# One quarter of a state-space product moved from VectorE to GpSimd, and the first expert tile fetched in the routing stage, in a fused Mamba, attention and mixture-of-experts kernel

## The chip, the cores and the metric

The kernel runs on one NeuronCore of a Trainium2 chip. The metric is the device time of one execution in microseconds (us); lower is better. In the text PE is TensorE, DVE is VectorE, ACT is ScalarE, POOL is GpSimd and SP is SyncE, which here only issues DMAs. SBUF is the on-chip memory of 128 partitions, PSUM the accumulators that TensorE writes.

## The reference

All arrays are float32. The input is x, 2 sequences of 2048 rows of 256. It is normalised, and the output is x plus the sum of two branches. Cut to what matters:

```python
# branch 1: state-space layer (512 inner channels, 16 states)
dA  = jnp.exp(jnp.einsum('bld,dn->bldn', dt, A))
dBx = jnp.einsum('bld,bln->bldn', dt, Bm) * xs[..., None]
h   = dA_t * h + dBx_t                      # a scan over the 2048 rows
y   = jnp.einsum('bdn,bn->bd', h, C_t)
out = ((y + xs * D) * jax.nn.silu(res)) @ W_out

# branch 2: attention (16 heads of 16), then one of 8 experts per row
x   = x + (o @ wo + bo)
hn2 = _layernorm(x, ln2_g, ln2_b)
idx = jnp.argmax(hn2 @ gate_w + gate_b, axis=-1)
y   = relu(hn2 @ w1[idx] + b1[idx]) @ w2[idx] + b2[idx]
return x + y
```

## The kernel before

The kernel is one program of five stages, one after the other, each a block with its own instruction stream for every engine: projections, the state-space layer, attention, routing, experts. Engines signal each other by semaphores. A stage ends when all engines have ended theirs. The order of the work on every engine is written out by hand.

**State-space stage (`phase_mamba`).** The 4096 rows are 8 chunks of 512. In a chunk there are 16 units k: unit k = (q, j) holds four states (group q of 4) of 128 channels (tile j of 4). All its tiles are 128 partitions (channels) by 4 x 512 (states by rows). One unit goes through the engines like this:
- POOL makes DB = B rows times U (dt times x), L1138, one unit or more ahead. Before that it makes the carry HS of the unit that DVE has finished (L1112), so it waits for DVE's product of unit k-2 (`hc_done`).
- ACT makes the decays exp(dt*A) for one state at a time into PSUM (L1243), two buffers deep.
- DVE runs four scans into H (L1521), then the product G = H * C rows over all four states (L1534), which signals `hc_done`. G, H and DB have two buffers each.
- PE adds the four states up in PSUM by four matmuls with the identity (L1387), which signals `y_done`.

In units 11 to 15 POOL also issues six DMAs that add into DT in memory (`add_steps`, L1124) and so form the next chunk's dt; some of them wait until an earlier one has landed. DVE makes U = dt * x for the next chunk in units 14 and 15 (L1480), and the gating product of one channel tile, read from PSUM, in units 13 to 15 and in unit 0 of the next chunk (L1488). PE runs the convolutions and projections of the next chunk in between. SP loads the rows of B and C, spread over all partitions (`load_b`, `load_c`).

**Routing stage (`phase_route`).** POOL first builds the identity and SEL, a 16 x 256 mask that spreads the softmax sums over the channels (L1663 to L1668). For each of 8 chunks PE projects, DVE normalises and picks the expert, and POOL scatters the rows' ids into the table ids_d, sorted by expert (L1688). Then DVE works out TE and TR, the expert and the first table row of each of 23 tiles (L1867 to L1884), and POOL waits until all scatters have landed.

**Expert stage (`phase_experts`).** For each tile of 256 rows SP loads ids, W1, B1, W2 and BB by the numbers in TE and TR (L1936 to L1955), POOL gathers the rows by the ids (L1981), PE transposes them (L2010) and multiplies by W1 (L2025) and W2 (L2038). Two buffers of weights, three of rows, four of ids. The stage begins with six memsets of the row buffers on DVE, for which the first gathers wait.

In the attention stage (`phase_attention`) POOL starts with memsets and six loads of weights, waits for them, and then has the first of 32 small casts (L756).

## Time and profile before

| | |
|---|---|
| median of 3 runs | 3058.38 us (3058.3 to 3058.73) |
| profiled execution | 3059.3 us, of which the span from the first to the last instruction is 3057.6 us |
| mean granted clock of PE | 0.959 of full speed |
| busy, share of the span | PE 93%, DVE 83%, ACT 57%, POOL 33% |
| state-space stage | about 190 to 1150 us |
| attention, routing, experts | from about 1163, 2582 and 2704 us |

The stages follow one another, so a change in one is worth what it does to that stage's own length. The profile gives every instruction with its start, its duration and, where its engine was idle before it, what ended the wait. A row that holds several instructions of one kind ends with their number.

### The profile page before, as it was taken

To read this page: it belongs to the slowest core of one execution; us is meant where nothing else is said; L and a number is where in the kernel's file an instruction comes from. 1 tells how busy PE (TensorE), PEld (TensorE's weight loads), DVE (VectorE), ACT (ScalarE), POOL (GpSimd) and SP (SyncE) were. 2 spreads that over 40 slices of the span, in tenths; PEclk is the share of its full clock that TensorE was granted. 3 is DMA by queue.
4 is the path that set the end of the run, shared out by engine and by line. 5 is a ranking of instruction groups with operands and counts; after the bars stand their busy time and mean duration, and the time that the engine had idled before them with its cause. 6 is when DMAs were issued, how large, how long until landed. Compare 5 with 4: busy or idle time off the path is not lost. (4 is left out here: it accounts for less than half of the span.)

```text
span 3057.6 us, 36491 instructions
## 1 busy us (share of the span) xinstructions
PE 2847.3 (93%) x13168; PEld 1457.7 (48%) x13168; DVE 2543.2 (83%) x4091; ACT 1757.2 (57%) x2146; POOL 1001.2 (33%) x652
## 2 busy tenths in 40 slices
PE   7988999989999668999999999999999998959998
PEld 4533434434434234444444444444444442758887
DVE  7569999999999997899999999999999993732222
ACT  4457567566676530677777777777777776111110
POOL 3337667666666753011010110101000000444443
PEclk9999999999999885899999999999999999779999
DMA  7624244343352526554465545655455501546663
GB/s 239 215 90 111 83 117 108 93 117 105 92 129 79 122 54 89 65 76 75 62 88 74 76 75 63 88 74 76 75 63 74 74 11 39 123 144 200 206 201 108
DMA packets 193968, 310.11 MB, mean 101 GB/s; under 512 B 97613, under 2 KB 133990, under 8 KB 179324
## 3 DMA queue, kind: packets, MB, share of 16 engines
q1 hardware_dynamic: 176380, 260.12, 39.9%
q0 software_dynamic: 17408, 47.66, 6.6%
q8 instruction: 104, 1.70, 0.2%
q14 instruction: 76, 0.62, 0.1%
HBM read 237.10 MB, written 53.52 MB: 95 GB/s over the span
## 5 line engine op out<-in xcount | busy, mean ns | idle before, releaser
L895 DVE TENSOR_REDUCE attn_mx<-attn_pX 128x1 f32<-128x512 f32 (+1 forms) x2560 | 1308.0, 576 | 52.7 <-PE attn_pX L798 14.7
L869 ACT ACTIVATE attn_pr<-attn_pS 128x1024 f32<-128x1024 f32 x1024 | 991.6, 1021 | 410.5 <-PE attn_pS L810 410.5
L798 PE MATMUL attn_pX<-attn_ks,attn_qs 48*128 48x512 f32 (+1 forms) x1920 | 660.9, 430 | 6.1 <-DVE attn_mx L895 5.1
L1521 DVE TENSOR_TENSOR_SCAN mamba_h<-mamba_pA,mamba_hs,mamba_db 128x512 f32<-128x512 f32 x512 | 616.8, 1264 | 13.0 <-ACT mamba_pA L1243 12.6
L1387 PE MATMUL mamba_pY<-mamba_g,mamba_ident 128*128 128x512 f32 x1024 | 498.0, 631 | 107.6 <-DVE mamba_g L1534 107.4
L1138 POOL TENSOR_TENSOR mamba_db<-mamba_bq,mamba_u 128x2048 f32<-128x2048 f32 x128 | 580.6, 4537 | 11.6 <-DVE mamba_u L1480 11.6
L798 PEld LDWEIGHTS attn_pX<-attn_ks,attn_qs 48*128 48x128 f32 x1920 | 327.9, 186 | 466.9 <-DVE attn_mx L895 412.4
L1243 ACT ACTIVATE mamba_pA<-mamba_dt,held_an 128x512 f32<-128x512 f32 x512 | 352.1, 690 | 295.2 <-DVE mamba_h L1521 292.5
L810 PE MATMUL attn_pS<-attn_qs,attn_ks 50*128 50x512 f32 x1536 | 466.0, 434 | 2.8 <-ACT attn_pr L869 2.8
L820 PE MATMUL attn_pO<-attn_pr,attn_vs 128*17 128x512 f32 x3072 | 404.2, 598 | 0.8 <-ACT attn_pr L869 0.7
L1387 PEld LDWEIGHTS mamba_pY<-mamba_g,mamba_ident 128*128 128x128 f32 x1024 | 194.0, 199 | 403.2 <-issue 203.7
L756 POOL CAST attn_ms<-attn_mn 128x16 fp32r<-128x16 f32 x32 | 6.3, 198 | 1146.9 <-DVE attn_mn L903 996.1
L1534 DVE TENSOR_TENSOR mamba_g<-mamba_h,mamba_bq 128x2048 f32<-128x2048 f32 x128 | 297.6, 2325 | 11.8
L798 PE MATMUL attn_pX<-item_ks,item_qs 48*128 48x512 f32 (+1 forms) x640 | 231.6, 460 | 11.4 <-DVE attn_mx L895 5.1
L810 PEld LDWEIGHTS attn_pS<-attn_qs,attn_ks 50*128 50x128 f32 x1536 | 215.3, 185 | 25.3 <-ACT attn_pr L869 24.4
L2087 DVE TENSOR_SCALAR exp_hm<-exp_pH,exp_b 128x256 f32<-128x256 f32 x46 | 22.3, 484 | 235.3 <-PE exp_pH L2025 235.3
L1331 PE MATMUL mamba_pP<-held_xt,held_wc 128*128 128x512 f32 x448 | 204.0, 599 | 3.1 <-ACT mamba_dt L1190 3.1
L2051 ACT ACTIVATE exp_hm<-exp_pH,exp_b 128x256 f32<-128x256 f32 x46 | 21.8, 475 | 317.3 <-PE exp_pH L2025 317.3
L798 PEld LDWEIGHTS attn_pX<-item_ks,item_qs 48*128 48x128 f32 x640 | 115.3, 196 | 167.7 <-DVE attn_mx L895 144.6
L2025 PE MATMUL exp_pH<-exp_xt,exp_w 128*128 128x256 f32 x736 | 165.7, 384 | 1.1 <-DVE exp_xt L2066 1.1
L2038 PE MATMUL exp_pY<-exp_w,exp_hm 128*128 128x256 f32 x736 | 162.7, 379 | 0.0
L810 PE MATMUL attn_pS<-item_qs,item_ks 50*128 50x512 f32 x512 | 157.9, 439 | 0.8 <-ACT attn_pr L869 0.8
(239 smaller groups left out, 2569.2 us busy)
## 6 DMA issues: line engine op xcount, KB each, us to landing
mamba_bq<-bc_d SPq DMA_DIRECT2D x64, 1024.0 KB, 5.3
exp_w<-in_w SPq DMA_DIRECT2D x46, 1024.0 KB, 5.5
attn_ks<-parts_d SPq DMA_DIRECT2D x144, 256.0 KB, 8.9
parts_d<-proj_qp SPq DMA_DIRECT2D x32, 512.0 KB, 5.7
attn_vs<-v_d SPq DMA_DIRECT2D x24, 544.0 KB, 16.0
item_ks<-parts_d SPq DMA_DIRECT2D x48, 256.0 KB, 9.4
attn_qs<-parts_d SPq DMA_DIRECT2D x144, 64.0 KB, 8.4
oraw_d<-attn_oe SPq DMA_DIRECT2D x32, 256.0 KB, 2.1
```

The lines of the kernel that those rows point to most:

```text
L798: pe.matmul(pX[bank(s, e)][:, 0:width], QS[slot][rows, pair, qt * P:(qt + 1) * P], KS[slot][rows, pair, keys:keys + width], start=True, st ...
L810: mm = pe.matmul(pS[pair][:, h, :], KS[slot][rows, pair, kt * P:(kt + 1) * P], QS[slot][rows, pair, :], start=True, stop=True)
L820: mm = pe.matmul(pO[32 * h:32 * h + VW, :], VS[s][:, kt, h, :], PR[2 * (kt % 2) + h // 2][:, h % 2, :], start=(kt == 0), stop=(kt == KT - 1))
L869: act.activation(PR[2 * (kt % 2) + pair][:, :, :], pS[pair][:, :, :], ACT.Exp, scale=HD ** -0.5).then_inc(p_sb, 1)
L895: dve.tensor_reduce(MX[s % 2][:, col, a:a + 1], pX[bank(s, e)][:, 0:width], AX.X, ALU.max).then_inc(x_max, 1)
L1138: pool.tensor_tensor(DB[k % 2][:, :, :], BQ[q % 2][:, 0, :, :], U[s][:, j, :].unsqueeze(1).to_broadcast([P, QN, BANK]), ALU.mult).then_inc ...
L1243: act.activation(pA[n % 2][:, :], DT[s][:, j, :], ACT.Exp, scale=AN[:, j, q * QN + n:q * QN + n + 1]).then_inc(da_done, 1)
L1331: mm = pe.matmul(bank(par, place)[:, :], WC[:, k, a, w], XT[sx][:, k, a:a + BANK], start=(k == 0 and a == 0), stop=(k == KC - 1 and a == T ...
L1387: mm = pe.matmul(pY[j][:, :], ident[:, :], G[k % 2][:, n, :], start=False, stop=(q == NQ - 1 and n == QN - 1))
L1521: dve.tensor_tensor_scan(H[k % 2][:, n, :], pA[n % 2][:, :], DB[k % 2][:, n, :], HS[:, j, q * QN + n:q * QN + n + 1], ALU.mult, ALU.add).t ...
L1534: dve.tensor_tensor(G[k % 2][:, :, :], H[k % 2][:, :, :], BQ[q % 2][:, 1, :, :], ALU.mult).then_inc(hc_done, 1)
L2025: mm = pe.matmul(pH[n][:, f % 2, :], W1[s][:, k, f * P:(f + 1) * P], XT[s][:, k, :], start=(k == 0), stop=(k == KC - 1))
```

## The change

In the state-space stage the product with C is split: DVE makes states 1 to 3 of the four, and state 0 is made by a new function on POOL, `first_of_four`, one unit later in POOL's order, behind DB. A new semaphore `hc_pool` tells of it. PE waits for it before its first matmul of the unit and for `hc_done` before the second; SP waits for both before it loads new rows of C.

SEL is built by POOL in the attention stage, behind its wait for the weights, and kept. In the routing stage the tiles of the first expert tile are placed, DVE clears two of them, and SP fetches W1 and B1 as soon as TE is there, then waits for the scatters and fetches ids, W2 and BB; POOL gathers the first 256 rows of hn. The expert stage takes these tiles over, with the identity, and loads only tile 1 and later ones.

```diff
# attention, POOL
                 pool.wait_ge(w_in, 16 * 6)
+                pool.memset(SEL[:, :, :], 1.0).then_inc(ones_ready, 1)
+                pool.wait_ge(ones_ready, 9)
+                pool.affine_select(out=SEL[:, :, :], in_=SEL[:, :, :], compare_op=ALU.is_gt, fill=0.0, base=1,
+                                   pattern=[[P, C // P], [1, P]], channel_multiplier=-HD).then_inc(ones_ready, 1)
...
# state-space stage
                 def load_c(c, q):
                     sp.wait_ge(hc_done, c * UNITS + (q * JT + JT))
+                    sp.wait_ge(hc_pool, c * UNITS + (q * JT + JT))
...
+                def first_of_four(c, k):
+                    q, j = divmod(k, JT)
+                    if j == 0:
+                        pool.wait_ge(c_in[q % 2], c * 32 + (16 * (q // 2) + 16))
+                    pool.wait_ge(y_done, c * UNITS + (k + 1))
+                    pool.wait_ge(scanned, c * SCANS + (k * QN + 3))
+                    pool.tensor_tensor(G[k % 2][:, 0, :], H[k % 2][:, 0, :], BQ[q % 2][:, 1, 0, :], ALU.mult
+                                       ).then_inc(hc_pool, 1)
...
                         pool.tensor_tensor(DB[k % 2][:, :, :], BQ[q % 2][:, 0, :, :],
                                            U[s][:, j, :].unsqueeze(1).to_broadcast([P, QN, BANK]), ALU.mult
                                            ).then_inc(db_done, 1)
+                        if k >= 1:
+                            first_of_four(c, k - 1)
+                        elif not first:
+                            first_of_four(c - 1, UNITS - 1)
                         if k == 3 and last:
...
                 bodies(pool, body)
+                first_of_four(NCH - 1, UNITS - 1)
...
-                        pe.wait_ge(hc_done, c * UNITS + (k + 9))
+                        pe.wait_ge(hc_pool, c * UNITS + (k + 9))
                         for n in range(QN):
+                            if n == 1:
+                                pe.wait_ge(hc_done, c * UNITS + (k + 9))
...
-                        dve.tensor_tensor(G[k % 2][:, :, :], H[k % 2][:, :, :], BQ[q % 2][:, 1, :, :], ALU.mult
+                        dve.tensor_tensor(G[k % 2][:, 1:, :], H[k % 2][:, 1:, :], BQ[q % 2][:, 1, 1:, :], ALU.mult
                                           ).then_inc(hc_done, 1)
...
# routing, SP, behind the stores of the last chunk
+                sp.wait_ge(consts, 11)
+                e = sp.value_load(TE[0:1, 0:1], min_val=0, max_val=NE - 1)
+                sp.dma_start(W1[:, :, :], w1[ds(e, 1), :, :].rearrange(...)).then_inc(w1_in, 16)
+                sp.dma_start(B1[:, :], b1[ds(e, 1), :, :].rearrange(...)).then_inc(w1_in, 16)
+                r = sp.value_load(TR[0:1, 0:1], min_val=0, max_val=ids_d.shape[0] - MT)
                 for n in range(2):
                     sp.wait_ge(hn_out[n], 16 * (NCH // 2))
                 sp.wait_ge(base_out, 16 * NCH)
+                sp.wait_ge(sent, 16 * NCH * TG)
+                sp.dma_start(ID[:, :, :]..., ids_d[ds(r, MT), :]...).then_inc(ids_in, 16)
+                sp.dma_start(W2[:, :, :], w2[ds(e, 1), :, :].rearrange(...)).then_inc(w2_in, 16)
+                sp.dma_start(BB[:, :], b2[ds(e, 1), :].to_broadcast([P, C])).then_inc(w2_in, 16)
...
# routing, POOL
-                pool.memset(SEL[:, :, :], 1.0).then_inc(id_ready, 1)
...
                 pool.wait_ge(sent, 16 * NCH * TG)
+                pool.wait_ge(ids_in, 16)
+                pool.wait_ge(consts, 10)
+                for t in range(TT):
+                    pool.indirect_dma_start(out=XR[:, t, :], out_offset=None, in_=hn_d, ...).then_inc(x_in, 16)
...
# routing, PE
-                pe.wait_ge(id_ready, 5)
                 spread(0)
                 project(0)
                 spread(1)
+                pe.wait_ge(id_ready, 2)
...
# experts
-                load_ids(0)
-                load_w(0)
                 load_ids(1)
                 load_w(1)
```

## Rows read from the trace of the kernel before

**Rows 1.** Busy time by stretch: us, PE, PEld, DVE, ACT, POOL, PEclk, DMA, GB/s.
```profile
190.00:1150.00 960.00, 852.36 (x1963) 368.86 (x1962) 938.07 (x687) 598.22 (x789) 627.76 (x295) 0.97 0.37 99
...
2697.00:2717.00 20.00, 1.09 (x4) 0.71 (x4) 3.19 (x7) 0.00 (x0) 5.46 (x7) 0.50 0.50 153
```

**Rows 2.** Timeline of one unit, DVE and POOL: start us, us, engine, line.
```profile
606.09 2.29 DVE L1534 TENSOR_TENSOR mamba_g<-mamba_h,mamba_bq 128x2048 f32<-128x2048 f32 x1
...
608.30 4.80 DVE L1521 TENSOR_TENSOR_SCAN mamba_h<-mamba_pA,mamba_hs,mamba_db 128x512 f32<-128x512 f32 x4
...
608.46 0.20 POOL L1112 TENSOR_TENSOR mamba_hs<-mamba_h,mamba_mk 128x4 f32<-128x4 f32 x1 [2.44 <-DVE mamba_g L1534]
...
608.61 4.52 POOL L1138 TENSOR_TENSOR mamba_db<-mamba_bq,mamba_u 128x2048 f32<-128x2048 f32 x1
...
613.23 2.29 DVE L1534 TENSOR_TENSOR mamba_g<-mamba_h,mamba_bq 128x2048 f32<-128x2048 f32 x1
```

**Rows 3.** Timelines of POOL and DVE where a product met DB.
```profile
638.46 4.84 POOL L1138 TENSOR_TENSOR mamba_db<-mamba_bq,mamba_u 128x2048 f32<-128x2048 f32 x1
...
641.73 3.73 DVE L1534 TENSOR_TENSOR mamba_g<-mamba_h,mamba_bq 128x2048 f32<-128x2048 f32 x1
...
1052.61 4.52 POOL L1138 TENSOR_TENSOR mamba_db<-mamba_bq,mamba_u 128x2048 f32<-128x2048 f32 x1
...
1056.25 3.03 DVE L1534 TENSOR_TENSOR mamba_g<-mamba_h,mamba_bq 128x2048 f32<-128x2048 f32 x1
```

**Rows 4.** Timelines of POOL and DVE in the projection stage.
```profile
80.86 2.49 POOL L220 TENSOR_TENSOR held_wc<-held_wc,proj_cw 128x512 f32<-128x512 f32 x2
...
83.29 0.68 DVE L518 TENSOR_TENSOR proj_qp<-proj_qf,proj_qp 128x512 fp32r<-128x512 f32 x1
...
83.31 2.41 POOL L201 TENSOR_TENSOR proj_hn<-proj_x,proj_rstd 128x1024 f32<-128x1024 f32 x1
...
83.89 2.38 DVE L518 TENSOR_TENSOR proj_qp<-proj_qf,proj_qp 128x512 fp32r<-128x512 f32 x1
```

**Rows 5.** One line's instructions: duration ns min/median/max, first and last start.
```profile
L220 POOL TENSOR_TENSOR held_wc<-held_wc,proj_cw x8: 1258/1270/1723, 67.7 to 108.8; 128x512 f32<-128x512 f32 x8
```

**Rows 6.** Timeline of DVE: dt*x of two chunks, and a scan that waited.
```profile
298.60 1.20 DVE L1480 TENSOR_TENSOR mamba_u<-mamba_dt,held_xs 128x1024 f32<-128x1024 f32 x1
...
702.03 2.46 DVE L1521 TENSOR_TENSOR_SCAN mamba_h<-mamba_pA,mamba_hs,mamba_db 128x512 f32<-128x512 f32 x2 [0.37 <-ACT mamba_pA L1243]
...
1017.06 1.20 DVE L1480 TENSOR_TENSOR mamba_u<-mamba_dt,held_xs 128x1024 f32<-128x1024 f32 x1
```

**Rows 7.** POOL's accumulating DMAs of one chunk, and all landings of L1124.
```profile
627.35 0.86 POOL L1124 DMA_DIRECT2D mamba_dt<-held_e  x1
...
637.73 0.86 POOL L1124 DMA_DIRECT2D mamba_dt<-mamba_u  x1 [3.21 <-DMA mamba_dt<-held_e]
...
DMA to landing us min/median/max: 4.5/6.9/10.2
```

**Rows 8.** Timelines: POOL's first cast of the attention, the start of routing.
```profile
1211.14 0.20 POOL L756 CAST attn_ms<-attn_mn 128x16 fp32r<-128x16 f32 x1 [23.10 <-DVE attn_mn L903]
...
2581.63 0.21 POOL L92 MEMSET route_ident<- 128x128 f32 x1 [45.08 <-POOLq L659]
...
2583.52 3.78 PE L1710 MATMUL route_pS<-rows_inv,route_sel 16*128 16x512 f32 x4 [5.14 <-POOL route_sel L1668]
```

**Rows 9.** The last scatter and its landing, then the chain that ended last.
```profile
2696.89 0.97 POOL L1688 DMA_INDIRECT ids_d<-route_idt,route_slot  x1 [0.30 <-issue]
...
DMA to landing us min/median/max: 4.2/4.2/4.2
...
2705.15 1.72 DMA exp_id<-ids_d
...
2709.09 6.37 DMA exp_xr<-hn_d,exp_id
...
2717.77 10.15 PE exp_pH L2025 x32
```

More of the change, by code:

```diff
@@ L578, in phase_attention @@
     NIDS = ids_d.shape[0] // P
-    WO, GW, GBI, G2, B2, XN, XB, INVA, OT0 = kept
+    WO, GW, GBI, G2, B2, XN, XB, INVA, OT0, SEL = kept
     NCH, TG, C = len(XN), BANK // P, XN[0].shape[2]
@@ L1540, in _, with phase_route @@
                 bodies(dve, body)
-def phase_route(nc, kept, oraw_d, rs_d, ids_d, hn_d, base_d, TE, TR, batches):
-    WO, GW, GBI, G2, B2, XN, XB, INVA, OT0 = kept
+def phase_route(nc, kept, oraw_d, rs_d, ids_d, hn_d, base_d, TE, TR, w1, b1, w2, b2, first_in, batches):
+    WO, GW, GBI, G2, B2, XN, XB, INVA, OT0, SEL = kept
     T, C = hn_d.shape
@@ L1564, in phase_route @@
         OT = [OT0] + [m.sb(f"ot{c}", [P, KC, BANK]) for c in range(1, NCH)]
-        SEL = m.sb("sel", [HEADS, KC, P])
         INVB = m.sb("inv", [HEADS, NCH - NB, BANK])
@@ L1583, in phase_route @@
         CMP = m.sb("cmp", [P, NTL, NE])
+        F = w1.shape[2]
+        KF, TT = F // P, MT // P
+        ids_in, x_in, w1_in, w2_in = first_in
+        m0 = Place(nc, ctx, "tile0")
+        ident = m0.sb("ident", [P, P])
+        W1, W2 = m0.sb("w1", [P, KC, F]), m0.sb("w2", [P, KF, C])
+        B1, BB = m0.sb("b1", [P, KF]), m0.sb("bb", [P, C])
+        ID = m0.sb("id", [P, TT, 2], I32)
+        XR, BX = m0.sb("xr", [P, TT, C]), m0.sb("bx", [P, TT, C])
         pA = m.ps("pA", [P, TG, C])
@@ L1851, in _ @@
                 chain.step(dve.tensor_copy(WTT[:, :, :], WT[:, :].unsqueeze(1).to_broadcast([P, TG, NE])))
+                dve.memset(XR[:, :, :], 0.0).then_inc(consts, 1)
+                dve.memset(BX[:, :, :], 0.0).then_inc(consts, 1)
                 for c in range(NCH):
@@ L1883, in _, with phase_experts @@
                 chain.step(dve.tensor_scalar(TEF[:, :], TEF[:, :], float(NE - 1), None, ALU.min))
-                chain.step(dve.tensor_copy(TE[:, :], TEF[:, :]))
-def phase_experts(nc, w1, b1, w2, b2, ids_d, hn_d, base_d, out, G2, B2, TE, TR):
+                dve.tensor_copy(TE[:, :], TEF[:, :]).then_inc(consts, 1)
+    return W1, W2, B1, BB, ID, XR, BX, ident
+def phase_experts(nc, first_tile, first_in, w1, b1, w2, b2, ids_d, hn_d, base_d, out, G2, B2, TE, TR):
     E, C, F = w1.shape
@@ L1910, in phase_experts @@
         pY = [m.ps(f"pY{n}", [P, TT, C]) for n in range(2)]
-        id_ready = m.sem("id_ready")
         cleared = m.sem("cleared")
-        ids_in = [m.sem(f"ids_in{n}") for n in range(RI)]
-        x_in = [m.sem(f"x_in{n}") for n in range(RX)]
+        ids_in = [first_in[0]] + [m.sem(f"ids_in{n}") for n in range(1, RI)]
+        x_in = [first_in[1]] + [m.sem(f"x_in{n}") for n in range(1, RX)]
         base_in = [m.sem(f"base_in{n}") for n in range(RX)]
-        w1_in = [m.sem(f"w1_in{s}") for s in range(2)]
-        w2_in = [m.sem(f"w2_in{s}") for s in range(2)]
+        w1_in = [first_in[2], m.sem("w1_in1")]
+        w2_in = [first_in[3], m.sem("w2_in1")]
         x_ps = m.sem("x_ps")
@@ L1976, in gather @@
                         pool.wait_ge(y_sum, j - RX + 1)
-                    else:
-                        pool.wait_ge(cleared, 2 * j + 2)
-                    for dst, src, done in ((XR, hn_d, x_in), (BX, base_d, base_in)):
+                    elif j >= 1:
+                        pool.wait_ge(cleared, 2 * j)
+                    for dst, src, done in ((XR, hn_d, x_in), (BX, base_d, base_in))[j == 0:]:
                         for t in range(TT):
@@ L2057, in _ @@
             def _(dve):
-                for n in range(RX):
+                for n in range(1, RX):
                     dve.memset(XR[n][:, :, :], 0.0).then_inc(cleared, 1)
@@ L2182, in build_layers @@
         TR = m.sb("tr", [P, NTL], I32)
+        first_in = [m.sem(n) for n in ("ids_in0", "x_in0", "w1_in0", "w2_in0")]
         with ExitStack() as rows:
```

45 lines of the change are left out of this document (25 added, 20 removed).

## The prediction, made before the changed kernel had run

> **What bounds the kernel now.** I read the busy time by stage first, then the timeline of the state-space stage engine by engine, then the single rows of its collisions, and last the chain of waits where the expert stage starts. The state-space stage runs from about 190 to 1150 us, and in it VectorE (DVE) is busy 938 of 960 us, TensorE 852, GpSimd (POOL) 628 [rows 1]. So DVE sets the pace, and the part moved off it looks like pure gain. The reader is to see in the timeline of one unit why it isn't [rows 2]. A unit is four scans (4.80 us), then the product with C (2.29 us), and the next unit's product starts 7.14 us later (7.12 in its neighbours). POOL waits for the end of the product at 608.38, does its carry of 0.20 us and then DB, which lasts 4.52 us and ends at 613.13. That is 0.10 us before the next product starts. The two engines are nearly in step: POOL works under the scans, DVE's product runs when POOL is idle.
>
> Whether they could overlap instead is seen where they did by accident [rows 3]. At 641.73 DVE's product met a DB that ran until 643.30: it lasted 3.73 us, not 2.29, and ended 2.16 us after DB. At 1056.25 it met a DB that ended at 1057.13 and ended itself at 1059.28, 2.15 us after it. Five more products in the same trace, longer than 2.31 us, end by the same rule. So a DVE product that reads two tensors in SBUF stands still while a POOL product runs, and has done only about 0.13 us of its work by then. Scans, whose decays come from PSUM, do not stand still: four last 4.80 us over a whole DB.
>
> The Trainium skill, page "SBUF — State Buffer", section "SBUF: two separate sides", says the same as a rule: GpSimd and a DVE instruction with two SBUF inputs share a port pair under an exclusive lock, and whichever starts first keeps it for its whole instruction. By that rule alone the moved quarter can't run beside the remaining three.
>
> **The state-space stage after the change.** Removed from each of 128 units: a quarter of DVE's product. A 512-column product took 0.68 us [rows 4] and a 2048-column one 2.29, so 1536 columns take 2.29 - 512 x (2.29-0.68)/1536 = 1.75 us; DVE alone would save 0.54 us a unit, 69 us in all.
>
> Added on POOL, behind DB in its program order: one product of 128x512. The nearest row is POOL's 128x512 product of the projection, median 1.27 us [rows 5]; a quarter of DB is 1.13, the lower bound; I take 1.27 and 1.4 as the upper one. It waits for y_done and for scan 0 of the unit, both long past when DB ends, so it starts at once, at about 613.1 in the unit shown, ahead of the product at 613.23. The product then stands still until POOL's quarter ends.
>
> The unit, from one product's end to the next: 0.08 us to wake POOL, 0.15 carry, 4.52 DB, 1.27 for the quarter less 0.04 overlap, then 1.75 - 0.13 for the rest of the product: 7.60 us against 7.12. Without the quarter DVE would be at its product after 4.83 us and finish after 6.58. The quarter costs 1.02 us of standing still and saves 0.54.
>
> The order of the two doesn't rescue it. In the projection stage a DVE product issued at 83.29, while POOL was busy until 83.35, went ahead of the POOL product issued at 83.31; that one ended at 85.72, and the next DVE product, issued at 83.89, ended only at 86.27 [rows 4]. The earlier request wins. If DVE's product goes first, POOL's quarter comes after it and delays the next carry and DB, so that the next product finds DB still running: 0.15 + 4.52 + 1.62 + 1.14 = 7.43 us. POOL's work and DVE's product add up in either order.
>
> A chunk of 16 units lasts now (1017.06 - 298.60)/6 = 119.7 us [rows 6]. After: 16 x 7.60 = 121.6. The two products dt*x also read two SBUF tensors and stay in the chain: 2 x 1.11 = 2.2. The four gating products (0.60 each, from PSUM) and two waits of scans for ScalarE (0.37 each) are now covered by the 1.0 us in which DVE waits anyway: nothing, which would be 3.1 us a chunk if that cover were gone. The accumulating DMAs on POOL's queue lie in units 11 to 15. The second is issued 10.4 us after the first, on its landing, and until then POOL stands: it delays the next DB by some 1.2 us [rows 7]. The last two are issued later relative to DVE, so that dt*x can wait for them: an issue moved behind the delayed quarter comes 1.1 us after the product, with landing after 4.5 to 10.2 us, against 4.8 us of scans; I allow 2 us a chunk. Bounds for both together are 0 and 6 us, I take 3.2. Sum 127.0, less 119.7: +7.3 us a chunk, for seven chunks +51. The last chunk has no such DMAs: 15 units more by 0.4 us, the last less by 0.5 since no DB stands before its quarter, four gating products covered (-2.4), a POOL memset behind unit 3's quarter some +0.5: +3. TensorE gets its first quarter early, about -1 at the very end. State-space stage: +53, of which I keep +51, since some units behind a delayed DB run in the 7.43 us order (some 15 units by 0.17).
>
> TensorE stays under this: 852 us of work in what becomes a longer stage. The two added semaphores are waited for by SP (C rows are loaded once both engines are done) and by TensorE; both are reached by DVE's product last, as now.
>
> **The rest of the change.** SEL is built before the attention instead of at the start of routing. There its three POOL instructions (about 1.1 us) stand behind the wait for weights, and POOL idles there for 23.1 us before its first cast [rows 8]: nothing; without that cover 1.1 us once. In routing TensorE's first matmul waits until 2583.52 for SEL, in a stage whose first instruction is at 2581.63 [rows 8]; it can start about 1.7 us sooner, and the chain of spread, scale and projection with it: -1.7, bounds 0 and -2. The two memsets that DVE gets in routing lie where it waits for the first projection; uncovered they would cost 1 us once.
>
> The first expert tile. Now the last scatter of the ids is issued at 2696.89 and lands 4.2 us later, at 2701.1; then the stage changes, and the ids are fetched at 2705.15 (1.72 us), the second gather is issued at 2709.09 and lands 6.37 us later beside the weights, and the first wide matmul starts at 2717.77 [rows 9]. After: W1 and B1 go out on SP as soon as the expert number is there, about when that scatter is issued, the ids at about 2701.3, landing at 2703 to 2704, POOL's two gathers at about 2704 and 2705.3, landing 4 to 6.4 us later: 2710.5 against 2715.46. So -5; bounds: -2, if ids and gathers queue behind W1 and W2 on the same engines or the stage change waits for the gathers, and -7. SP's queue then holds W2 and BB behind the wait for the scatters, which TensorE needs only after the 10.15 us of the first tile. Later tiles are bound by TensorE and keep their time.
>
> The first tile stays cold: the granted clock is 0.50 from 2697 to 2717, the lower of the two levels (1.2 GHz), with TensorE busy 1.09 of 20 us [rows 1]. A pause shorter by 5 us is still a pause of over 15 us: nothing gained.
>
> **Sum.** The profiled execution took 3059.3 us, 1.7 above its span and 0.9 above the median of the runs. 3059.3 + 51 - 1.7 - 5 = 3103.6; less 0.9 for the median: 3103 us, 1.5% slower.
>
> **The rivals.**
> 1. No standing still: POOL's quarter runs beside the product, because it is short or because it is issued together with it. Then a unit takes 4.83 + 1.75 = 6.58 us, and POOL's 6.0 us fit into it. 128 x 0.54 = -69; given back are longer waits for ScalarE, which already stops a scan now and then [rows 6], and waits of dt*x for the DMAs, together 3 to 4 us a chunk, +26. With -6.7 from the rest: 3009 us. It is faster if a quarter delays the product by less than 0.54 us; every one of the seven collisions cost the whole overlap less 0.13. Chance 7%. By the lock rule of the Trainium skill's page "SBUF — State Buffer" it could not happen.
> 2. The quarter loses each race: with the 1.1 us after the product also the six DMA issues of 0.86 us [rows 7] lie in the chain, and 5 us of landings: 16 x 7.43 + 2.2 + 5.2 + 5 = 131.3, +11.6 a chunk, 3135 us. For it speaks that the earlier request wins and that late units stay late; against it, that the 0.1 us lead of POOL comes back with each unit in which DVE arrives later (dt*x). Chance 6%.
> 3. Only the edges count: the state-space stage ends nearly even, the covered gating products and scan waits (3.1 us a chunk) and a quarter of 1.13 us paying for most of the loss, and the DMA allowance is zero. Per chunk 16 x 7.46 + 2.2 = 121.6, +1.9; with +1 in the last chunk 3066 us. Chance 4%, and 1% more that it comes within 0.2% (6 us, which is about what a measurement of this kernel can tell).
>
> **How the numbers follow.** Forecast 82%. Its range: a quarter of 1.13 instead of 1.27 us takes 18 us away, one of 1.4 adds 17; the DMA allowance moves it by -22 or +20; the expert tile by 3. These are independent, so about -25 and +22: 3078 to 3125. Left out are rival 1 (7%), most of rival 2 and rival 3, and some of the forecast's tails. Slower by over 0.2%: 0.91; within: 0.02; faster: 0.07.
>
> **What would show it.** Right: the product of DVE, now 1536 columns, lasts about 2.8 us and not 1.75, and ends 1.6 us after POOL's quarter; the distance of two products is 7.4 to 7.6 us; scans don't wait for ScalarE any more; a chunk takes 126 to 128 us; the first wide matmul of the experts starts 5 us sooner after the last scatter. Wrong: products of 1.75 us, units of 6.6 us (rival 1); a POOL quarter far from 1.27 us; dt*x starting without a wait, which puts a chunk at 124 us; or ids landing late behind W1.

## The result, and the profile after the change

The changed kernel takes 3080.74 us (median of four runs, 3079.6 to 3083.37) against 3058.34 us of the kernel before beside it on the same chip (3055.55 to 3058.73): ratio 1.0077, 95% interval 1.0064 to 1.0089. It is slower by 22.4 us (19.6 to 27.2 by that interval). The forecast was 3103 us, +44.7 on the median shown. The sign and the main mechanism held, the size was twice too large, and the time lies in the forecast's range, 2.7 us above its lower end.

The profiled execution took 3079.71 us, with a span of 3078.0 us, 20.4 more than before. The state-space stage comes first. This is the timeline of one unit of the changed kernel, DVE and then POOL, the counterpart of [rows 2] (start us, us, engine, line, operation):

```profile
604.91 2.77 DVE L1561 TENSOR_TENSOR mamba_g<-mamba_h,mamba_bq 128x1536 f32<-128x1536 f32 x1
607.60 4.80 DVE L1548 TENSOR_TENSOR_SCAN mamba_h<-mamba_pA,mamba_hs,mamba_db 128x512 f32<-128x512 f32 x4
612.50 2.77 DVE L1561 TENSOR_TENSOR mamba_g<-mamba_h,mamba_bq 128x1536 f32<-128x1536 f32 x1
...
607.75 0.20 POOL L1122 TENSOR_TENSOR mamba_hs<-mamba_h,mamba_mk 128x4 f32<-128x4 f32 x1 [1.69 <-DVE mamba_g L1561]
607.90 4.52 POOL L1158 TENSOR_TENSOR mamba_db<-mamba_bq,mamba_u 128x2048 f32<-128x2048 f32 x1
612.38 1.27 POOL L1132 TENSOR_TENSOR mamba_g<-mamba_h,mamba_bq 128x512 f32<-128x512 f32 x1
```

The two products of DVE are 7.59 us apart. POOL's quarter begins at 612.38, 0.12 us ahead of DVE's product, and ends at 613.65. The product begins at 612.50 and ends at 615.27, 1.62 us after the quarter. It has three quarters of its old columns and lasts 0.48 us longer. The last product of the stage has no POOL work beside it, and there the same 1536 columns take 1.76 us, in the timeline of the changed kernel:

```profile
1174.36 1.76 DVE L1561 TENSOR_TENSOR mamba_g<-mamba_h,mamba_bq 128x1536 f32<-128x1536 f32 x1
```

Over the whole stage the groups by line of the changed kernel say the same (busy us, mean ns of one, then idle time before them):

```profile
L1548 DVE TENSOR_TENSOR_SCAN mamba_h<-mamba_pA,mamba_hs,mamba_db 128x512 f32<-128x512 f32 x510 | 611.4, 1256 | 0.0
...
L1561 DVE TENSOR_TENSOR mamba_g<-mamba_h,mamba_bq 128x1536 f32<-128x1536 f32 x128 | 327.5, 2559 | 11.7
```

No scan waits for ScalarE any more. A chunk is read as before from the two ends of a row of dt*x (timeline of DVE, changed kernel), where [rows 6] had 119.7 us:

```profile
302.30 1.86 DVE L1507 TENSOR_TENSOR mamba_u<-mamba_dt,held_xs 128x1024 f32<-128x1024 f32 x1
...
1044.97 1.82 DVE L1507 TENSOR_TENSOR mamba_u<-mamba_dt,held_xs 128x1024 f32<-128x1024 f32 x1
```

(1044.97 - 302.30) / 6 = 123.8 us, +4.1 a chunk, where the forecast had 127.0. The end of the last product moved from 1145.95 to 1176.12 us, +30.2.

The accumulating DMAs are where the forecast and the trace part. POOL's timeline, and the landings of line 1144, answer to [rows 7]:

```profile
643.94 0.84 POOL L1144 DMA_DIRECT2D mamba_dt<-held_e  x1
645.69 0.19 POOL L1122 TENSOR_TENSOR mamba_hs<-mamba_h,mamba_mk 128x4 f32<-128x4 f32 x1 [0.91 <-DVE mamba_g L1561]
...
651.55 0.84 POOL L1144 DMA_DIRECT2D mamba_dt<-mamba_u  x1
...
DMA to landing us min/median/max: 4.5/5.8/7.3
```

The second is issued 7.6 us after the first, behind its own unit's quarter, and waits for nothing. Before, it was issued 10.4 us after it and POOL had stood for 3.21 us.

At the other end of the kernel, the last scatter, the fetches of the first expert tile and its first matmuls (timelines of POOL, SP and TensorE, changed kernel), for [rows 9]:

```profile
2719.71 0.97 POOL L1724 DMA_INDIRECT ids_d<-route_idt,route_slot  x1 [0.30 <-issue]
...
2720.64 0.41 SPq L1692 DMA_DIRECT2D tile_w<-in_w  x1
...
2724.28 0.34 SPq L1699 DMA_DIRECT2D tile_id<-ids_d  x1
...
2730.17 1.05 POOL L1737 DMA_INDIRECT tile_xr<-hn_d,tile_id  x1 [9.49 <-issue]
2731.53 1.02 POOL L1737 DMA_INDIRECT tile_xr<-hn_d,tile_id  x1 [0.31 <-issue]
...
2736.12 1.09 PE L2050 MATMUL exp_pT<-tile_ident,tile_xr 128*128 128x128 f32 x4 [21.38 <-PEq L1650]
```

The ids are asked for at 2724.28 and POOL's first gather goes out at 2730.17; their landing took 5.0 us, where it had been 1.72. The first wide matmul starts at 2739.14, 19.4 us after the last scatter was issued, against 20.9 before: 1.5 us less in this pair of traces, where 5 were forecast. The first tile then takes 9.20 us against 10.15. The traces of the experiments show, further below, that neither difference stands out of the spread between executions.

### The profile page after: what moved, and what is told of

Same layout as the page of the kernel before. It is cut to its first block and busy times, and to the rows that moved or that the text cites. A ratio compares the mean times of both kernels' runs of the same rounds, so it can differ in the third digit from the quotient of the medians.

```text
span 3078.0 us, 36773 instructions
## 1 busy us (share of the span) xinstructions
PE 2857.8 (93%) x13168; PEld 1454.0 (47%) x13168; DVE 2578.5 (84%) x4091; ACT 1757.6 (57%) x2146; POOL 1174.2 (38%) x778
## 5 line engine op out<-in xcount | busy, mean ns | idle before, releaser
L1414 PE MATMUL mamba_pY<-mamba_g,mamba_ident 128*128 128x512 f32 x1024 | 522.8, 641 | 122.4 <-POOL mamba_g L1132 61.2
L1561 DVE TENSOR_TENSOR mamba_g<-mamba_h,mamba_bq 128x1536 f32<-128x1536 f32 x128 | 327.5, 2559 | 11.7
L1132 POOL TENSOR_TENSOR mamba_g<-mamba_h,mamba_bq 128x512 f32<-128x512 f32 x128 | 180.9, 1413 | 0.8 <-DVE mamba_h L1548 0.8
L1356 PEld LDWEIGHTS mamba_pP<-held_xt,held_wc 128*128 128x128 f32 x448 | 85.7, 192 | 113.5 <-issue 108.6
L827 PE MATMUL attn_pO<-attn_pr,item_vs 128*17 128x512 f32 x1024 | 135.6, 602 | 0.0
L2126 DVE TENSOR_SCALAR exp_hm<-exp_pH,tile_b 128x256 f32<-128x256 f32 x24 | 11.6, 483 | 121.5 <-PE exp_pH L2064 114.4
```

The lines of the kernel that those rows point to most:

```text
L827: mm = pe.matmul(pO[32 * h:32 * h + VW, :], VS[s][:, kt, h, :], PR[2 * (kt % 2) + h // 2][:, h % 2, :], start=(kt == 0), stop=(kt == KT - 1))
L1132: pool.tensor_tensor(G[k % 2][:, 0, :], H[k % 2][:, 0, :], BQ[q % 2][:, 1, 0, :], ALU.mult).then_inc(hc_pool, 1)
L1356: mm = pe.matmul(bank(par, place)[:, :], WC[:, k, a, w], XT[sx][:, k, a:a + BANK], start=(k == 0 and a == 0), stop=(k == KC - 1 and a == T ...
L1414: mm = pe.matmul(pY[j][:, :], ident[:, :], G[k % 2][:, n, :], start=False, stop=(q == NQ - 1 and n == QN - 1))
L1561: dve.tensor_tensor(G[k % 2][:, 1:, :], H[k % 2][:, 1:, :], BQ[q % 2][:, 1, 1:, :], ALU.mult).then_inc(hc_done, 1)
```

## The experiments

Twelve kernels ran. Four ran once, with a profile, beside one run of the kernel before (3058.39 us); I read them by their units. The others were timed against the kernel before, whose median was 3059.55 us beside runs 5 to 8 and 3058.97 us beside runs 9 to 12.

**1. No quarter.** In the changed kernel:

```diff
-                    pool.tensor_tensor(G[k % 2][:, 0, :], H[k % 2][:, 0, :], BQ[q % 2][:, 1, 0, :], ALU.mult
-                                       ).then_inc(hc_pool, 1)
+                    pool.sem_inc(hc_pool, 1)
```

> The changed kernel with GpSimd's quarter left out: state 0 of G is zeroed once and TensorE multiplies zeros, so the term of every fourth state with C is missing from the output. DVE keeps its 128x1536 product. Theory (POOL's product and DVE's product with two SBUF inputs add up): with nothing of POOL behind DB, the product lasts 1.75 us instead of 2.56 and the unit falls from 7.60 to 4.83 + 1.75 = 6.58 us, some 6.7 with waits of scans for ScalarE; the accumulating DMAs are issued earlier again, so a chunk keeps 1 to 4 us at its edge: about 3080.7 - 128 x 0.95 + 15 = 2975 us. Rival (DVE's product is slow for another reason, its shape or the two semaphores added): the product stays near 2.56 us and the unit near 7.6, time about 3080.

3005.96 us. The timeline of DVE shows products of 1.76 us at a distance of 6.58 us:

```profile
599.82 1.76 DVE L1561 TENSOR_TENSOR mamba_g<-mamba_h,mamba_bq 128x1536 f32<-128x1536 f32 x1
601.50 4.80 DVE L1548 TENSOR_TENSOR_SCAN mamba_h<-mamba_pA,mamba_hs,mamba_db 128x512 f32<-128x512 f32 x4
606.40 1.76 DVE L1561 TENSOR_TENSOR mamba_g<-mamba_h,mamba_bq 128x1536 f32<-128x1536 f32 x1
```

So neither the shape nor the added semaphores make the product slow; POOL's quarter does. The time is 31 us above my 2975: a chunk has 113.5 to 115.0 us, 113.9 in the mean, of which 16 x 6.58 = 105.3. The other 8.6 us had too small an allowance. With nothing to wait for under DVE, the gating products, the waits for ScalarE (16.4 us over the stage) and the DMAs' landings (POOL waited 28.0 us for them) come out. It is rival 1 of the prediction in effect, with the quarter left out instead of hidden, and that was priced at 3009.

**2. Two memsets in its place.**

```diff
+                    pool.memset(G[k % 2][:, 0, :], 0.0).then_inc(hc_half, 1)
+                    pool.wait_ge(hc_half, c * UNITS + (k + 1))
+                    pool.memset(G[k % 2][:, 0, :], 0.0).then_inc(hc_pool, 1)
```

> The changed kernel with POOL's quarter replaced by two dependent memsets of the same 512 columns (about 1.1 to 1.3 us in all), so state 0 of G is zero and its term is missing from the output. POOL is about as long behind DB as with the quarter, but reads nothing from SBUF. Theory (DVE's product stands still only while POOL reads SBUF tensors): the product lasts 1.75 us, the unit is set by DVE at 6.6 to 6.8 us, time 2975 to 3000 us. Rival (whatever POOL executes behind DB holds the product, or the order of the semaphores does): the product lasts about 2.5 us and the unit stays at 7.5 us, time about 3075.

3004.76 us. Timelines of POOL and DVE:

```profile
600.27 0.52 POOL L1133 MEMSET mamba_g<- 128x512 f32 x1
600.84 0.53 POOL L1135 MEMSET mamba_g<- 128x512 f32 x1
...
600.40 1.76 DVE L1563 TENSOR_TENSOR mamba_g<-mamba_h,mamba_bq 128x1536 f32<-128x1536 f32 x1
...
606.98 1.76 DVE L1563 TENSOR_TENSOR mamba_g<-mamba_h,mamba_bq 128x1536 f32<-128x1536 f32 x1
```

POOL is busy from 600.27 to 601.37, about as long as the quarter, and the product beside it takes 1.76 us. Work of POOL that only writes doesn't hold it. The rival of this run is out.

**3. A copy in its place**, one input from SBUF.

```diff
+                    pool.tensor_copy(G[k % 2][:, 0, :], H[k % 2][:, 0, :]).then_inc(hc_pool, 1)
```

> The changed kernel with POOL's quarter replaced by a copy of state 0 of H to G (128x512, one SBUF input): C is left out of every fourth state's product. Theory A: POOL's copy holds the product as its multiplication does, only for the copy's own length: if the copy takes 0.6 to 0.9 us the unit is 7.60 - 1.27 + that, 6.9 to 7.3 us, and the time 3080.7 less 128 times the difference, 2995 to 3040. Rival: an operation of POOL with one SBUF input doesn't hold DVE's product at all: product 1.75 us, unit 6.6 to 6.8, time 2975 to 3000.

3020.14 us. Timelines of POOL and DVE:

```profile
608.97 0.61 POOL L1132 COPY mamba_g<-mamba_h 128x512 f32<-128x512 f32 x1
...
609.11 2.08 DVE L1560 TENSOR_TENSOR mamba_g<-mamba_h,mamba_bq 128x1536 f32<-128x1536 f32 x1
```

The copy ends at 609.58 and the product at 611.19, 1.61 us later: the same distance as behind the multiplication. The unit is 6.91 us, and 7.59 less the 0.66 us by which the copy is shorter gives 6.93. Reading one tensor is enough.

**4. Half instead of a quarter.**

```diff
-                    pool.tensor_tensor(G[k % 2][:, 0, :], H[k % 2][:, 0, :], BQ[q % 2][:, 1, 0, :], ALU.mult
+                    pool.tensor_tensor(G[k % 2][:, :2, :], H[k % 2][:, :2, :], BQ[q % 2][:, 1, :2, :], ALU.mult
...
-                        dve.tensor_tensor(G[k % 2][:, 1:, :], H[k % 2][:, 1:, :], BQ[q % 2][:, 1, 1:, :], ALU.mult
+                        dve.tensor_tensor(G[k % 2][:, 2:, :], H[k % 2][:, 2:, :], BQ[q % 2][:, 1, 2:, :], ALU.mult
```

> Two of the four states' products on POOL (128x1024) and two on DVE (128x1024); the whole computation. Theory (the two products add up, whatever the split): POOL's part 2.36 to 2.54 us, DVE's 1.22, so the unit is 0.08 + 0.15 + 4.52 + 2.40 - 0.04 + 1.22 - 0.13 = 8.2 us, some 0.6 more than with a quarter: 3080.7 + 128 x 0.6 = 3158 us. Rival (the loss is a fixed cost of the hand-over between the engines, about 0.5 us a unit whatever the size): the unit becomes 7.60 - 0.53 + at most 0.1 = 7.1 to 7.2 us and the time about 3025.

3155.64 us, where 3158 was expected and 3025 by the rival. Timelines of POOL and DVE:

```profile
603.59 2.35 POOL L1132 TENSOR_TENSOR mamba_g<-mamba_h,mamba_bq 128x1024 f32<-128x1024 f32 x1
...
603.71 3.30 DVE L1561 TENSOR_TENSOR mamba_g<-mamba_h,mamba_bq 128x1024 f32<-128x1024 f32 x1
...
611.83 3.32 DVE L1561 TENSOR_TENSOR mamba_g<-mamba_h,mamba_bq 128x1024 f32<-128x1024 f32 x1
```

A unit is 8.12 us here, and 8.10 to 8.16 in most of the stage. The loss grows with the columns moved: half costs more than a quarter, so it is no fixed cost of handing over.

**5. The state-space part alone**, on the kernel before: of the change only first_of_four with its calls and waits, and

```diff
-                        dve.tensor_tensor(G[k % 2][:, :, :], H[k % 2][:, :, :], BQ[q % 2][:, 1, :, :], ALU.mult
+                        dve.tensor_tensor(G[k % 2][:, 1:, :], H[k % 2][:, 1:, :], BQ[q % 2][:, 1, 1:, :], ALU.mult
```

> The kernel before with only the state-space part of the change (POOL's quarter); the select matrix and the first expert tile as before. Theory (the changed kernel's ledger): the state-space stage gives +30.2 less 2.6 behind it, the rest about -4.1 to -4.9 and is missing here, so 3058.3 + 27 = 3085 us, 3083 to 3087. Rival (the rest of the change brings nothing, or costs something): 3081 or less, as the changed kernel.

3086.86 us (3082.85 to 3087.54), ratio 1.0088 (1.0072 to 1.0103). The stage's last product ends at 1175.99 us, as in the changed kernel (1176.12). The whole loss is here: 27.3 us over the kernel before, where the whole change costs 22.4.

**6. The rest alone**: the changed kernel with the old state-space stage.

```diff
-                        if k >= 1:
-                            first_of_four(c, k - 1)
-                        elif not first:
-                            first_of_four(c - 1, UNITS - 1)
...
-                        dve.tensor_tensor(G[k % 2][:, 1:, :], H[k % 2][:, 1:, :], BQ[q % 2][:, 1, 1:, :], ALU.mult
+                        dve.tensor_tensor(G[k % 2][:, :, :], H[k % 2][:, :, :], BQ[q % 2][:, 1, :, :], ALU.mult
```

> The changed kernel with the old state-space stage: only the select matrix built earlier and the first expert tile fetched in routing. Theory: routing's first matmul 1.8 us sooner, the first wide matmul of the experts 1.5 us sooner and its tile 0.9 us shorter: 3058.3 - 4.3 = 3054 us, ratio 0.9986. Rival (the shorter first tile and the 2.7 us of the attention belong to the state-space change or are run-to-run): ratio 0.9990 to 1.0000.

3057.96 us (3054.76 to 3060.07), ratio 0.9997 (0.9988 to 1.0006). The theory's 0.9986 lies outside the interval, and the rival's 0.9990 to 1.0000 holds: what the rest brings, 1.6 us in the medians, is too small for this measurement. Runs 5 and 6 together give +25.7 us, inside the interval of the whole change. In the trace of run 6 only the first of the two savings is plain. Routing's first matmul starts 0.04 us behind POOL's first instruction of the stage, where it was 1.9 behind [rows 8]. The first wide matmul starts at 2714.07, 20.6 us after the last scatter (20.9 before). Timelines of POOL and DVE, and the landing of the gathers:

```profile
2693.43 0.97 POOL L1704 DMA_INDIRECT ids_d<-route_idt,route_slot  x1 [0.30 <-issue]
2705.14 1.05 POOL L1717 DMA_INDIRECT tile_xr<-hn_d,tile_id  x1 [10.74 <-issue]
2706.49 1.01 POOL L1717 DMA_INDIRECT tile_xr<-hn_d,tile_id  x1 [0.31 <-issue]
DMA to landing us min/median/max: 2.8/2.8/2.8
...
2711.18 0.48 DVE L2078 MEMSET exp_xr<- 128x512 f32 x1 [17.87 <-PEq L1630]
...
2712.80 0.48 DVE L2079 MEMSET exp_bx<- 128x512 f32 x1
2713.21 0.36 DVE L2084 TENSOR_SCALAR exp_xt<-exp_pT,kept_g,kept_b 128x256 f32<-128x256 f32 x1
```

Between the last scatter and the first gather lie 11.7 us. All engines change stage at about 2711, and then DVE clears four buffers of later tiles ahead of the scaling that TensorE waits for.

The distance from the last scatter to the first wide matmul can be read in seven traces with this code: 19.4 us in the changed kernel, 20.5, 21.4, 22.0 and 21.2 in runs 1 to 4, 20.6 here and 21.3 in run 8. The old code has 20.9 in the kernel before, 21.2 in run 5 and 21.8 in run 9. So the 1.5 us of the result section are the best of seven traces, and no gain by this fetch is shown.

**7. The ids ahead of the weights.** SP's loads of W1 and B1 stand behind the load of the ids.

```diff
-                sp.dma_start(W1[:, :, :], w1[ds(e, 1), :, :].rearrange("e (k p) f -> p (e k) f", p=P)).then_inc(w1_in, 16)
-                sp.dma_start(B1[:, :], b1[ds(e, 1), :, :].rearrange("e p k -> (e p) k")).then_inc(w1_in, 16)
...
                 sp.dma_start(ID[:, :, :].rearrange("p t o -> p (t o)"), ids_d[ds(r, MT), :].rearrange("(p t) o -> p (t o)", t=TT)).then_inc(ids_in, 16)
+                sp.dma_start(W1[:, :, :], w1[ds(e, 1), :, :].rearrange("e (k p) f -> p (e k) f", p=P)).then_inc(w1_in, 16)
+                sp.dma_start(B1[:, :], b1[ds(e, 1), :, :].rearrange("e p k -> (e p) k")).then_inc(w1_in, 16)
```

> As the run with the old state-space stage and the rest of the change, but SP issues the load of W1 and B1 behind the load of the token ids instead of ahead of the scatters' wait. Theory (the ids land late because they share the queues with W1's 1 MB): the ids land after 1.7 to 2.5 us instead of 5.0, POOL's gathers go out about 3 us sooner and with them the change of stage, but W1 lands later, so that the first wide matmul waits for W1: it starts between 2 us sooner and 1 us later, time within 2 us of that run. Rival (the ids are late because their DMA itself is slow behind the scatters' landing): ids still 4 to 5 us, gathers at the same place, time 1 to 3 us longer for the later W1.

3055.91 us (3052.8 to 3057.32), ratio 0.9989 (0.9980 to 0.9998). Timelines of POOL and TensorE, and the landing of the gathers:

```profile
2694.69 0.97 POOL L1704 DMA_INDIRECT ids_d<-route_idt,route_slot  x1 [0.30 <-issue]
2702.52 1.05 POOL L1717 DMA_INDIRECT tile_xr<-hn_d,tile_id  x1 [6.86 <-issue]
2703.88 1.01 POOL L1717 DMA_INDIRECT tile_xr<-hn_d,tile_id  x1 [0.31 <-issue]
DMA to landing us min/median/max: 5.9/6.4/6.9
...
2711.54 1.09 PE L2030 MATMUL exp_pT<-tile_ident,tile_xr 128*128 128x128 f32 x4 [21.82 <-PEq L1630]
```

The ids land in 1.7 us, and the first gather goes out 7.8 us after the last scatter instead of 11.7: W1 had held them up, as the theory said. But the weights now meet the gathers. These land after 5.9 and 6.9 us, not 2.8, at 2709.4 and 2709.8, and the stage changes 1.8 us after that. The first wide matmul comes 19.9 us after the last scatter: 0.8 us better than run 6. Runs 10 and 11, with the same order, have 19.2 and 18.9, where the seven traces with W1 first have 19.4 to 22.0.

**8. The accumulating DMAs ahead of the quarter.** In POOL's loop body:

```diff
-                        if k >= 1:
-                            first_of_four(c, k - 1)
-                        elif not first:
-                            first_of_four(c - 1, UNITS - 1)
                         if k == 3 and last:
...
                         if k == 15 and not last:
                             add_steps(c, 1 - s, 1, LN, 2)
+                        if k >= 1:
+                            first_of_four(c, k - 1)
+                        elif not first:
+                            first_of_four(c - 1, UNITS - 1)
```

> The changed kernel with POOL's order turned in units 11 to 15: the accumulating DMA is issued ahead of the quarter, right behind DB, as in the kernel before. The computation is the same. Theory (what I had allowed 3.2 us a chunk for depends on the moment of issue: right behind DB the DMA meets SP's 1 MB load of B and lands after about 10 us, behind the quarter it lands after 6.6 us, within a unit): the landing goes back to 9 to 10 us, POOL waits 1.5 to 3 us for it once or twice a chunk, the quarter comes behind DVE's request in those units; a chunk grows by 1 to 3 us, time 3088 to 3100. Rival (the DMAs cost nothing because DVE's extra waiting time covers them wherever they are issued): a chunk stays at 123.8 us, time 3081.

3100.29 us (3098.03 to 3101.13), ratio 1.0134 (1.0119 to 1.0150). A chunk has 125.8 us, 2.0 more than in the changed kernel, 14 us over seven chunks; 3 us more come in the last chunk, where the same edit also puts the quarter behind a memset. Timelines of POOL and DVE:

```profile
644.65 4.54 POOL L1158 TENSOR_TENSOR mamba_db<-mamba_bq,mamba_u 128x2048 f32<-128x2048 f32 x1
649.12 0.85 POOL L1144 DMA_DIRECT2D mamba_dt<-held_e  x1
649.72 1.56 POOL L1132 TENSOR_TENSOR mamba_g<-mamba_h,mamba_bq 128x512 f32<-128x512 f32 x1
...
658.76 0.87 POOL L1144 DMA_DIRECT2D mamba_dt<-mamba_u  x1 [1.11 <-DMA mamba_dt<-held_e]
...
649.25 3.65 DVE L1561 TENSOR_TENSOR mamba_g<-mamba_h,mamba_bq 128x1536 f32<-128x1536 f32 x1
```

The first DMA is issued at 649.12, 0.14 us before SP's next load, and lands only after 9.1 us; the second goes out 9.6 us after the first. So the landing does depend on the moment, and POOL waits again, but 1.1 us a chunk and not 1.5 to 3. The rest of the 2.0 us comes in another way: the quarter starts 0.6 us later, the product still ends 1.62 us after it, and stands still the longer.

**9. The load of B later**, on the kernel before.

```diff
+                        sp.wait_ge(hc_done, (c + 1) * UNITS + JT)
                         load_b(c + 1, 0)
```

> The kernel before with one wait added on SP: its load of the next chunk's first B rows waits for the DVE product that follows DB, some 2.4 us, instead of for that DB alone; the accumulating DMA of unit 11 stays where it was. Theory (the DMA lands late because both loads are issued at the same moment): it lands after some 6.6 us instead of 9.9, POOL's wait of 3 us for it goes, unit 12 of a chunk falls from 8.6 to about 7.15 us, a chunk by 1.4, the time by 7 x 1.4 = 10 us: 3049, ratio 0.9967. Rival (the landing is late because of something else that happens at that moment, or the loads only move their collision): unit 12 stays at 8.4 to 8.6 us, ratio 0.999 to 1.001.

3057.84 us (3052.37 to 3061.07), ratio 0.9995 (0.9986 to 1.0004). The edit moved the load further than the 2.4 us that I had expected. The wait is for the product of the unit whose DB the load had followed, and that product ends one unit later. SP's timeline, one chunk, where the first accumulating DMA goes out at 629.21:

```profile
638.77 0.93 SPq L1031 DMA_DIRECT2D mamba_bq<-bc_d  x2
```

The load comes 9.6 us after that DMA, where it came 0.13 us after it at 627.48 in the kernel before: 9.4 us later, and 2.4 us behind the second DMA (636.34). The mechanism held and the size did not. The first DMA of a chunk now lands after 4.5 to 4.7 us instead of 8.6 to 9.9. POOL waits 0.5 us over the whole stage for these DMAs, where it waited 14.0, and the landings have a median of 5.2 us instead of 6.9, by line:

```profile
  DMA mamba_dt<-mamba_u: 0.5, 1
...
DMA to landing us min/median/max: 4.5/5.2/9.2
```

But a chunk falls only from a mean of 119.7 to 119.4 us. Four of the six chunks before had 119.4 to 119.6 us already; the two of 120.1 and 120.4, one of which [rows 7] show, were the exception. I took that chunk for typical in the expectation, as in the prediction.

**10. The four memsets behind the first tile's scaling**, on run 7.

```diff
-                for n in range(1, RX):
-                    dve.memset(XR[n][:, :, :], 0.0).then_inc(cleared, 1)
-                    dve.memset(BX[n][:, :, :], 0.0).then_inc(cleared, 1)
...
                 turned(0)
+                for n in range(1, RX):
+                    dve.memset(XR[n][:, :, :], 0.0).then_inc(cleared, 1)
+                    dve.memset(BX[n][:, :, :], 0.0).then_inc(cleared, 1)
```

> As the run with the ids ahead of the weights, and the four memsets with which DVE clears the buffers of expert tiles 1 and 2 stand behind the scaling of the first turned tile instead of ahead of it. Theory (they lie in the chain of the first tile by about 1 us): the first wide matmul starts 2.0 to 2.1 us after TensorE's turning starts instead of 3.0; time 1 us less than that run, ratio to the kernel before 0.9985 or so. Rival (turning ends late or the weights are awaited): still 3.0 us.

3056.53 us (3054.28 to 3058.21), ratio 0.9991 (0.9982 to 1.0000). From TensorE's first turning (2712.24) to its first wide matmul (2714.42) it is 2.18 us, against 3.03 in run 7. As expected in the trace; too small for the median.

**11. Runs 9 and 10 together**: both diffs, with the changed kernel's rest under them.

> The two runs before this one together: old state-space stage with SP's B load 2.4 us later, select matrix and first expert tile as in the changed kernel, ids ahead of the weights, memsets behind the first tile. Theory: the gains add up, -10 and -4: 3045 us, ratio 0.9954. Rival (the B load moves nothing): ratio 0.9985.

3052.11 us (3048.41 to 3055.09), ratio 0.9975 (0.9966 to 0.9985). This is faster than both kernels, by 7 us where I expected 14. The single parts gave -1.1 and -2.4 us in their medians; that the sum is more than their -3.6 is within the intervals.

**12. The gathers of the first tile in the expert stage**, on run 11.

```diff
-                for t in range(TT):
-                    pool.indirect_dma_start(out=XR[:, t, :], out_offset=None, in_=hn_d,
-                                            in_offset=bass.IndirectOffsetOnAxis(ap=ID[:, t, 0:1], axis=0),
-                                            bounds_check=T - 1, oob_is_err=False).then_inc(x_in, 16)
...
-                    for dst, src, done in ((XR, hn_d, x_in), (BX, base_d, base_in))[j == 0:]:
+                    for dst, src, done in ((XR, hn_d, x_in), (BX, base_d, base_in)):
```

> As the run with both, but POOL gathers the first tile's rows at the start of the expert stage, no longer in routing; ids and weights still come in routing. Theory (the stage can change only some 1.7 us after the gathers of routing have landed, so that TensorE finds its data at the change and not before): the stage changes 5 us or more sooner, but the gathers are then issued behind it and land 2.8 to 6 us later, so TensorE's first turning starts within 1.5 us of where it was, time the same. Rival (the stage change does not follow the gathers): the change stays where it was and the gathers behind it cost 4 to 7 us more, time +4 to +7.

3053.45 us (3049.43 to 3054.45), ratio 0.9978 (0.9969 to 0.9987): the time of run 11. Timelines of POOL and TensorE:

```profile
2687.89 0.97 POOL L1705 DMA_INDIRECT ids_d<-route_idt,route_slot  x1 [0.30 <-issue]
2699.22 1.05 POOL L1998 DMA_INDIRECT tile_xr<-hn_d,tile_id  x1 [10.36 <-POOLq L1631]
...
2706.63 1.11 PE L2027 MATMUL exp_pT<-tile_ident,tile_xr 128*128 128x128 f32 x4 [23.71 <-DMA tile_xr<-hn_d,tile_id]
```

The expert stage starts 11.3 us after the last scatter, in run 11 it was 16.7. So the change of stage does follow the gathers. Now TensorE waits for the gather itself, and its turning (the transposing of the rows) begins 18.7 us after the last scatter, 2.0 later than in run 11, a little outside my 1.5.

## Why the prediction was right in its sign and twice too large in its size

- **The unit.** Forecast 7.60 us from one product's end to the next: quarter 1.27, product 1.75 alone, about 2.8 beside the quarter, its end 1.62 us behind the quarter's. Measured 7.57 to 7.61, with 1.27, 1.76, 2.77 and 1.62. Runs 1 to 4 make the cause more than a reading. The product is back at 1.76 us when the quarter is gone, and stays there when POOL works without reading. It lasts 0.32 us longer beside a copy of 0.61, 1.01 longer beside the quarter of 1.27, and 2.08 longer beside a half of 2.35 (1024 columns alone take DVE 1.22 us, at the end of run 4): POOL's own time less 0.26 to 0.29 each time.
- **The lock rule of the Trainium skill.** In the page "SBUF — State Buffer", section "SBUF: two separate sides", the pair is contested by a DVE instruction with two SBUF inputs only against a GpSimd operation that reads SBUF. Runs 2 and 3 agree on both sides of that "only": memsets beside the product, 1.76 us; a copy beside it, 2.08.
- **The order.** The first seven chunks run in the order with the quarter first. The late order, forecast at 7.43 us, came in the last chunk, behind POOL's memset: 11 units of 7.35 to 7.37, again from end to end. The last chunk gave +2.1 us, forecast +3.
- **The covered work.** Gating products and waits for ScalarE inside DVE's standing time at no cost, and 2 x 1.11 us for dt*x: with 16 x 7.60 these give 123.8 us a chunk, and 123.8 was measured. Run 1 shows the same work come out again when the cover is gone.
- **The step that failed: "Bounds for both together are 0 and 6 us, I take 3.2"**, the allowance for the accumulating DMAs. It measured 0, the lower bound, and seven chunks make 22 of the 23.5 us by which the stage was missed (51 less the 27.5 below). The others nearly cancel: 0.9 in the last chunk, 1.7 in the tail, a start 0.8 us earlier, and the 2 us that I had already taken off. Even before, the allowance was too high: POOL waited 12.6 us in five of the seven chunks for such a landing, 2.5 us a time against the 3.21 of [rows 7], and 1.65 of these it idles there anyway (run 9). Behind the quarter the issue comes 1.1 us after the load, it lands in 6.6 us, and a unit of 7.6 us covers that. Run 8 puts the issue back ahead of the quarter and pays 2.0 us a chunk. Run 9 moves the load instead and takes the waits away. The prediction had this among its signs of being wrong: "dt*x starting without a wait, which puts a chunk at 124 us". A second of these signs, ids landing late behind W1, came true too.
- **The stage's end.** The last product ends 30.2 us later, and the attention's first cast (1238.6, [rows 8] had 1211.14) comes 62.5 us after it instead of 65.2, so 27.5 us of the stage reach the next one. The forecast was about -1 there, measured -2.7. TensorE does start on the quarter early, with 2 of the unit's 8 matmuls, but that is only half of it. The other half I had not seen: its granted clock. TensorE stood for 4.0 us before its last matmuls in the kernel before, and for 1.5 us in the changed one, and only the first came out of it at a lower clock (busy time by stretch, before and after, columns as in [rows 1]):

```profile
1146.00:1151.50 5.50, 5.40 (x8) 2.03 (x8) 0.61 (x2) 0.00 (x0) 0.00 (x0) 0.69 0.00 0
1176.00:1179.10 3.10, 2.84 (x6) 1.06 (x6) 0.76 (x3) 0.00 (x0) 0.00 (x0) 1.00 0.00 0
```

Eight matmuls took 5.40 us at a mean clock of 0.69, six take 2.84 at 1.00.
- **Attention.** From its first cast to the first instruction of routing it took 2.7 us less in the changed trace, 1367.8 against 1370.5. No term of the forecast stands for that. Between kernels with the same attention it varies by as much, 1367.6 us in run 6 and 1371.1 in run 10, so most of it can be scatter between executions. The two other traces with the old attention are at the top of the spread, 1371.7 in run 5 and 1371.8 in run 9, so a small gain by the change isn't excluded.
- **The select matrix.** Forecast -1.7, measured -1.85 us: first matmul 0.04 us behind POOL's first instruction instead of 1.9.
- **The first expert tile.** Forecast -5, bounds -2 and -7; the pair of traces has -1.5 us to the first wide matmul and -0.95 in its tile, -2.4 together. That it touches the bound is luck. The 1.5 us are the best of seven traces (run 6). The tile's length, from its first wide matmul to the turning of the next tile, is 10.0 us before and 9.0 after, but 8.9 in run 5 and 8.5 in run 9, which have the old expert stage. So no gain is shown for this term. Both reasons that I had named for the lower bound came true together. The ids landed late beside W1 (5.0 us; run 7: 1.7), and the stage change waited for the gathers (run 12). A third I had not seen: the four memsets, once in the shadow of the fetch, now lie in the chain (0.85 us, run 10).
- **The rivals.** The first (no standing still) is refuted by every unit. The second, the late order in all chunks, came only where the memset forced it. The third had the allowance right at zero, and the quarter wrong at 1.13 us.
- **The sum.** 3059.3 + 27.5 - 2.7 - 1.85 - 2.4 = 3079.9; the profiled execution took 3079.7. The median of runs is 1 us above it. The 2.7 and the 2.4 are not shown to come from the change. Without them the change costs 27.5 - 1.85 = 25.7 us, which is what runs 5 and 6 add up to, and still 19 us less than the forecast.

## What to carry to other kernels

Before work is moved from VectorE to GpSimd, look whether the VectorE instruction that stays behind reads two tensors in SBUF. If so, and GpSimd's instruction reads SBUF too, the two durations very nearly add up. GpSimd's is more than twice as long for the same columns (1.27 us against 0.54 here), and the move loses even though GpSimd is idle in a third of the stage. What did overlap here was GpSimd's work under scans fed from PSUM (DB of 4.52 us under four scans of 4.80), and memsets, which read nothing, beside the product (run 2).

An allowance for a DMA wait that was read in one row should be checked against the total of such waits before it is multiplied by the number of chunks. A fetch moved ahead of a stage change is worth only what the change does not give back: here it waited for the fetched data itself. And a gain of one or two microseconds read in one pair of traces should be looked up in every other trace with the same code, before it is put into a sum.

## What the runs showed of the hardware that I had not expected

- A GpSimd multiplication that started 0.5 us after VectorE's product had begun still went ahead of it when a DMA issue of GpSimd's stood between DB and the quarter (run 8). The product began at 649.25, 0.06 us after DB's end, and ended 1.62 us after the quarter, not 1.76 us plus a quarter after its own start. In run 1 the same DMA issue (606.29) with no quarter behind it left the product at 1.76 us. What decides between the two in that gap wasn't settled.
- An accumulating DMA that was issued within 0.2 us of SP's load of B rows landed after 9.0 to 9.2 us in run 8 and after 8.6 to 9.9 us in the kernel before, and after 6.5 to 7.2 us when it was issued 1.1 us behind that load (the changed kernel). With the load 9.4 us later it landed after 4.5 to 4.7 us, and the median of all landings went from 6.9 to 5.2 us (run 9).
- The change from one stage of the program to the next came 1.8 us after the last gather of GpSimd had landed (run 6: issued at 2706.49 and landed 2.8 us later, TensorE's first instruction at 2711.05; run 7: issued at 2703.88, landed 5.9 us later, TensorE at 2711.54).
